# The hand-over from self-attention to the rest of a decoder layer: a load, two sums, a weight split and one product change places

## The reference

```python
x = x + self_attention(layernorm(x))            # qkv, softmax over 1024 keys, out projection W_out, b_out
x = x + cross_attention(layernorm(x), ctx)      # Wq, Wk, Wv, Wo; 64 context rows per batch
x = x + ffn(layernorm(x))                       # h = gelu(x @ ternary(W_fc).T); layernorm(h)*ln_w+ln_b; @ ternary(W_proj).T
# ternary(W): gamma = mean|W| + 1e-6; sign(W) * min(round(|W| / gamma), 1)
```

## Time and profile before

| | |
|---|---|
| median of 3 runs | 1179.52 us (1178.5 to 1180.77) |
| the profiled execution | 1182.6 us; its span 1180.8 us |
| busy, share of the span | PE 96%, DVE 86%, ACT 75%, GpSimd 25% |
| chain that ended last, by engine | PE 75%, DVE 11%, ACT 8%, GpSimd 2% |
| mean granted clock of PE | 0.991 |

### The profile page before, as it was taken

One profiled execution on the slowest core, in us unless ns is written; L12 is line 12 of the kernel. 1 busy time (PEld: TensorE's weight loads), 2 busy tenths in 40 slices (PEclk: granted clock), 3 DMA queues, 4 the chain that ended last, 5 costly groups with the idle time before them and its releaser, 6 DMA issues.

```text
span 1180.8 us, 19363 instructions
## 1 busy us (share of the span) xinstructions
PE 1131.4 (96%) x6648; PEld 592.4 (50%) x6648; DVE 1019.7 (86%) x1909; ACT 885.5 (75%) x1958; POOL 299.6 (25%) x436
## 2 busy tenths in 40 slices
PE   8999999999999999999999999998789999999987
PEld 6544333333333333333333333343568778768767
DVE  5678899999999999999999999974588988988766
ACT  5312688878888888888888888865798889889853
POOL 2124010110110111011011000013665645645431
PEclk9999999999999999999999999998999999999999
DMA  5867122660430331233144000031211111100001
GB/s 180 270 207 233 72 38 33 146 120 11 65 60 7 65 60 32 39 60 51 21 64 65 9 11 8 15 105 50 74 35 40 55 56 35 55 19 19 2 19 36
DMA packets 45921, 75.00 MB, mean 64 GB/s; under 512 B 10112, under 2 KB 23808, under 8 KB 45824
## 3 DMA queue, kind: packets, MB, share of 16 engines
q0 software_dynamic: 9648, 27.27, 13.2%
q1 hardware_dynamic: 36176, 46.50, 13.1%
HBM read 47.53 MB, written 25.69 MB: 62 GB/s over the span
## 4 chain that ended last, share of the span: by engine, by line
PE 75%; DVE 11%; ACT 8%; issue 2%; POOL 2%; DMA 1%; SPq 1%; POOLq 0%; DVEq 0%; ACTq 0%
PE ps L1455 21%; PE ps L1442 21%; PE ps L1289 12%; PE ps L1328 11%; PE ps L1641 4%; DVE xhat L1182 3%; PE ps L1626 2%; DVE fstats L1169 2%; ACT pe_ L744 2%; PE ps L1558 2%; ACT ot L732 1%; ACT prob L669 1%; PE ps L1570 1%; ACT xn L772 1%; DVE maxes L927 1%
## 5 line engine op out<-in xcount | busy, mean ns | idle before, releaser
L934 DVE TENSOR_REDUCE maxes<-ps 128x1 f32<-128x512 f32 x968 | 607.0, 684 | 30.6 <-PE ps L1328 14.2
L669 ACT ACTIVATE prob<-ps 128x512 f32<-128x512 f32 x1024 | 531.6, 604 | 118.4 <-PE ps L1442 117.0
L1442 PE MATMUL ps<-Qs,Ks 50*128 50x512 f32 x1024 | 377.5, 452 | 3.8 <-ACT prob L669 1.4
L1328 PE MATMUL ps<-Ks,Qs 48*128 48x512 f32 x1024 | 320.9, 430 | 3.0 <-DVE maxes L927 2.6
L1442 PEld LDWEIGHTS ps<-Qs,Ks 50*128 50x128 f32 x1024 | 168.2, 185 | 309.4 <-ACT prob L669 297.5
L1455 PE MATMUL ps<-prob,V_all 128*32 128x512 f32 x2048 | 273.6, 606 | 0.0
L1328 PEld LDWEIGHTS ps<-Ks,Qs 48*128 48x128 f32 x1024 | 166.4, 186 | 49.9 <-DVE maxes L927 16.7
L358 POOL DMA_DIRECT2D Qs<-qk_scratch x90 | 44.4, 500 | 465.8 <-PE ps L1455 465.6
L744 ACT ACTIVATE pe_<-ps,nmx 128x64 f32<-128x64 f32 x512 | 109.5, 397 | 20.7 <-DVE nmx L1112 20.6
L582 POOL TENSOR_TENSOR pe_<-pe_,rsum 128x512 f32<-128x512 f32 x64 | 66.0, 1043 | 58.7 <-DVE rsum L1129 58.7
L656 ACT ACTIVATE parts<-ps,b_qk 128x512 fp32r<-128x512 f32 x32 | 22.0, 687 | 68.2 <-PE ps L1289 68.2
(11 more groups left out here) (127 smaller groups left out, 1246.6 us busy)
## 6 DMA issues: line engine op xcount, KB each, us to landing
qk_scratch<-parts SPq DMA_DIRECT2D x32, 512.0 KB, 5.2
Qs<-qk_scratch POOLq DMA_DIRECT2D x90, 128.0 KB, 5.2
Ks<-qk_scratch POOLq DMA_DIRECT2D x90, 128.0 KB, 7.5
o_scratch<-ot SPq DMA_DIRECT2D x128, 32.0 KB
on_raw<-o_scratch SPq DMA_DIRECT2D x8, 512.0 KB
r_raw<-r_scratch SPq DMA_DIRECT2D x16, 256.0 KB
x_in<-in_x SPq DMA_DIRECT2D x8, 512.0 KB, 5.3
out<-xo SPq DMA_DIRECT2D x8, 512.0 KB, 2.9
```

The costliest lines, as they stand in the source:

```text
L669: act.activation(prob[:, U % 2, j // 2, j % 2, :], ps[:, ST_BANK[n], :], ACT.Exp).then_inc(exp_done, 1)
L934: dve.tensor_reduce(maxes[:, qc, j * BLK + blk, half:half + 1], ps[:, MAX_BANK["tile", t], :], AX.X, ALU.max).then_inc(max_reduced, 1)
L1328: pe.matmul(ps[:, bank, :], stack(Qs[g], j, STACK, slice(q0, q0 + P)), stack(Ks[g], j, STACK, slice(half * 512, (half + 1) * 512)), start= ...
L1442: pe.matmul(ps[:, ST_BANK[n], :], stack(Ks[g], j, ROWS, slice(kb * P, (kb + 1) * P)), stack(Qs[g], j, ROWS, slice(qc * CH, (qc + 1) * CH)) ...
```

## The change

`load_xc(0)` is issued ahead of the last `m_rows` instead of behind `load_o(0, 0)`, with a wait for `pv_done` 240 in front. `x_plus_b(0)` becomes the first thing that GpSimd does in stage C, ahead of `normalise(0)`. `normalise(1)` gets a further wait, for `xn2_ready` 1, which is the end of DVE's four norms of chunk 0. On DVE the `kbd` steps, `b_q2` and `x1_half(0, 0)` come ahead of `t_split(1)`, and `x1_half(0, 1)` behind it. PE's `q2(0, 0)` waits for step 14 of the preparation instead of 16 (the `kbd` step in either order). ACT's wait for step 17 is left as it is: before, that step was `b_q2`, and now it is the end of `t_split(1)`.

```diff
--- before.py
+++ after.py
@@ -449,13 +449,14 @@
                         sp.wait_ge(recip_done, B - 1)
                         for i in range(B - 1):
                             r_write(i)
+                        sp.wait_ge(pv_done, UNITS * (GROUPS - 1))
+                        load_xc(0)
                     m_rows(2 * G + 1, g, 1)
                     if G == 2:
                         load_weights()
                     if last and g == NG - 1:
                         sp.wait_ge(r_written, 16 * (B - 1))
                         load_o(0, 0)
-                        load_xc(0)
                     o_write(G, b, g, 0)
                     if last and g == NG - 1:
                         next_loads(0)
@@ -527,6 +528,8 @@
                 pool.wait_ge(on_loaded, 16 * (1 + KT) * (c + 1))
                 if c:
                     pool.wait_ge(out_done, 2 * c)
+                if c == 1:
+                    pool.wait_ge(xn2_ready, 1)
                 pool.tensor_tensor(onT[:], on_raw[:], r_raw[:], ALU.mult).then_inc(o_normed, 1)
 
             def x_plus_b(c):
@@ -603,6 +606,7 @@
 
             pool.wait_ge(c_weights, C_LOADS)
             pool.wait_ge(minus_set, 1)
+            x_plus_b(0)
             for c in range(-2, NCH):
                 if c == 0:
                     pool.wait_ge(pv_done, GROUPS * UNITS)
@@ -623,7 +627,8 @@
                 normalise(c + 2)
                 rstd_f(c - 1, 2)
                 rstd_f(c - 1, 3)
-                x_plus_b(c + 2)
+                if c + 2 > 0:
+                    x_plus_b(c + 2)
 
             rstd_3(END)
             pool.wait_ge(xn3_ready, NCH)
@@ -1075,7 +1080,6 @@
                 n += 1
                 dve.wait_ge(prep_done, n)
 
-            t_split(1, w_p, t_p)
             dve.wait_ge(prep_mm, 4)
             for m in range(KT):
                 src = ps[:, 5, m * B * CTX:(m + 1) * B * CTX].rearrange("p (b t) -> p b t", b=B)
@@ -1087,8 +1091,9 @@
 
             dve.tensor_scalar(b_q2[:], b_q2[:], float(D) ** -0.5, None, ALU.mult).then_inc(prep_done, 1)
             n += 1
-            for k in range(2):
-                x1_half(0, k)
+            x1_half(0, 0)
+            t_split(1, w_p, t_p)
+            x1_half(0, 1)
             x1_stats(0)
             x1_apply()
             dve.tensor_tensor(lb[:], ln_b[:, :, None].broadcast_to([P, HT, P]),
@@ -1465,7 +1470,7 @@
                     if kind == "out":
                         pe.wait_ge(prep_done, 5 + 4 * (i + 1))
                     elif kind == "q2":
-                        pe.wait_ge(prep_done, PREP_STEPS - 3)
+                        pe.wait_ge(prep_done, PREP_STEPS - 5)
                     else:
                         pe.wait_ge(x1_added, i + 1)
                 if (kind, c, i) in BEFORE:
```

## The result

The changed kernel took 1174.95 us (median of 6 executions, 1172.84 to 1178.12) against 1180.62 for the kernel before (6 executions, 1178.5 to 1184.12): ratio 0.9955, 95% interval 0.9933 to 0.9976. By the ratio that is 5.3 us faster (the two medians are 5.7 us apart). The forecast was 7.0.

The account below looks back on a forecast made before the run. The bound at 776 to 806 was DVE's list, stretched by GpSimd's big sums and products. Gap 3.5 plus clock 3.8 made 7.3 us (1172.2 from the median 1179.5), taken as 7.0: 1172.5, range 1169.8 to 1175.4.

Parts of the forecast that it names:

- The gap goes whole: In front of `t2`: PE's wait of 3.52 us for `xn` vanishes, with 2.7 us to spare.
- `x_in` and the early sum: Ahead of stage C: earlier load and `x_plus_b(0)` shorten the `vbd` pair, moving DVE's list 2.1 us ahead.
- The four norms: DVE's `xn` of chunk 0: with `normalise(1)` behind them they fall from 5.46 to 1.37 us, 4.1 less.
- `lb` beside `normalise(1)`: DVE after the norms: `lb` at worst sits through both GpSimd operations until 805.9, with 3 us of cover.
- TensorE from 802.57 on: From `t2` to values of 255: these begin at 808.1 instead of 815.38, 7.3 us earlier.
- What is late next is ScalarE: Behind `t2`: ACT, busy with exponentials until 802.70, is late next; PE's gap there about 0.8 us.
- The clock: PE behind the gap, about 806 to 815: full clock instead of 1.2 GHz, 3.8 of the 7.3 us.
- A plain shift behind that: From cross-attention's start to the end: the remaining 365 us only shift, as nothing later has a fixed time.
- The clock that falls all the same: Rival, behind `t2`: low clock remains and only the gap goes, 3.5 us, 1176.0; chance 0.08.
- the contention that moves: Rival, DVE beside GpSimd's moved operations: PE idles 2 us, keeps the clock, gain 5.3, 1174.2; chance 0.05.
- the loss behind the tail: Rival: something later, for instance stage C's pipeline, gives the time back, 1179.5; chance 0.04.
- GpSimd's order: Rival: late `x_in` holds `x_plus_b(0)`, then `normalise(0)` and PE's `out_proj(0, 0)`; with 10 us more, 1186; chance 0.03.

Follow-up runs that it names:

- late_2: Changed kernel with the product that makes `lb` done two more times on VectorE between the reciprocal and the norms; ratio to the kernel before 0.9949.
- filler_14: Kernel before with 14 small matmuls of ones on TensorE in front of `t2`, in the wait for `xn`; ratio 0.9973.
- filler: Kernel before with 26 small matmuls of ones on TensorE in front of `t2`, behind a wait for `x1_added`; ratio 0.9995.

## Why the prediction was right, point by point

- *The gap goes whole.* Right. `xn` ended at 802.07 in after; less the 2.50 us by which stage A was later, 799.6, against 799.9. The cover was forecast as 2.7 and is 2.9, and late_2 used up 2.5 of it without moving the time.
- *`x_in` and the early sum.* `x_plus_b(0)` ran at 773.50, 771.0 in before's times (772.2 forecast), in idle time of VectorE. `r_raw` landed 1.2 us earlier (784.02 - 2.50 against 782.75), where I had said some tenths. The saving on the `vbd` pairs is 2.4 us, within my 1.1 to 3.
- *The four norms.* 1.38 us, 1.37 forecast. This one term was enough for the whole gain, which the text did not say though its numbers did: 806.05 - 4.1 = 802.0 lies ahead of 802.57. I added both savings and did not ask which of them crosses the line.
- *`lb` beside `normalise(1)`.* It did not wait: it started at 801.99, ahead of `onT` at 802.25, and took 1.22 us. GpSimd's `onT` did, 3.19 us instead of 2.44, and nobody needed it. The Trainium skill (GPSIMD Engine Reference, Key points) names the contention for an instruction with two SBUF inputs; the trace agrees that there is some, and shows that here GpSimd paid.
- *TensorE from 802.57 on.* Right term by term: transposes 1.0 us, `q2` 1.92 to the next start (1.81 forecast); the whole saved 7.21 against 7.28.
- *What is late next is ScalarE.* Right: 0.57 us of waiting, and 1.06 us of the tail when the order is changed.
- *The clock.* 3.8 us of the forecast. From `t2` to the values of unit 255 it was 9.28 us before and 5.67 after, 3.6 less; filler_14 shows 3.7 in the trace and 3.2 (1.3 to 5.2) in the time.
- *A plain shift behind that.* Right for the order of the work, and incomplete for the clock. I took the remaining 365 us as fixed. The dip of 830 to 840 in after and those in stage A come and go between executions of one and the same kernel, and they set how far one comparison lies from the next (5.3 and 8.2 us). In filler TensorE's rows start at the same times as in before, to 0.01 us, from 816.4 to 835.6, and yet the clock fell at 836 in filler (0.69 from 836 to 838, 0.50 from 838 to 842) and stayed at 1.00 in before. (The stretch from 806 to 815 differs: there before ran at 1.2 GHz and filler did not.)
- *The number.* The 7.0 for the median met the 6.8 between the medians of all executions. That the first comparison fell inside the range is in part luck: 1174.95 is 0.45 us from the upper bound, the kernel before itself measured 1180.62 there and not the 1179.52 that the sum starts from, and the gain of 5.3 was near the low bound of 5.2 for another reason than the one that I gave for that bound. It was not a short spell behind the gap but 1.2 GHz elsewhere, for which the forecast had no term. The lower end of the range is a slip besides: 1179.52 - 8.2 - 1.2 is 1170.1, not 1169.8.
- *The rivals.* The clock that falls all the same, the contention that moves, the loss behind the tail and GpSimd's order did not occur. In the traces the clock stayed behind a gap of 0.95 us ahead of `t2` and fell behind gaps of 2.16, 3.10 and 3.52 there. That is one profiled execution of each, and no threshold follows from it: between 830 and 845, where TensorE's waits are no longer than 1.6 us but many, it fell in some traces and not in others.

## What to carry to other kernels

When an instruction lasts several times as long as its kind does elsewhere, look at what the neighbour engine runs in that moment and whether both end together; then move the one that nobody waits for behind the other, with one wait. Sum the savings, but also ask which single one crosses the point where the waiting engine arrives: here one line did all, and the rest was cover. And price a gap of TensorE with the clock behind it: here half of what it cost was work at 1.2 GHz that filling the gap with idle matmuls gave back.

## What the runs showed of the hardware that I had not expected

- A `vbd`, `xn` or `xhat` that ran into a big GpSimd operation lasted until that operation was over, whatever its own length. Of the four norms before, the shortest took 0.40 us and the longest 2.45, and the last of them began at 805.6, when the product and the sum (2.44 and 2.39 us) were over; one `vbd`, half as wide, sat out a whole sum (2.43 us). With `lb` (two inputs in SBUF) it was the other way round: it ran at its own 1.22 us and GpSimd was stretched by 0.75. What these rows have in common is that the one that started first kept its length: `onT` at 915.53 ahead of `xhat` at 915.60, which then took 2.85 us, but `lb` at 801.99 ahead of `onT` at 802.25. No run turned the order round for one and the same pair, so this is a reading of the rows.
- The time of one execution follows its clock: 0.39 us for each us at 1.2 GHz, over 168 executions of 13 kernels. The scatter within a kernel is 2.1 us without that line and 1.1 with it, so the granted clocks sharpen a comparison of the times. The Trainium skill (TensorE: Matmul & The Clock Gate, Terms) gives the penalty as about the throttled time times one minus the ratio of the clock, which makes 0.5 us for each us at half clock, an estimate. The runs say 0.39, and so does the tail: the 9.28 us behind the gap, at clock 0.51, became 5.67, 3.6 less, with TensorE waiting 0.57 us for ScalarE in them. That such waits are the reason everywhere is likely and was not tested.
- The 26 fp32 matmuls of 128 x 128 by 128 x 128 of filler are 52 entries in the timeline, one about every 0.115 us; the eight transposes of `t2` are eight.
